# Slots of a hand-staged pipeline: 46 entries of the table AT are set to other numbers

## The reference

```
x = x + attn(norm(x))      # softmax((x*w_lhs)(x*w_rhs)^T) x, per sequence
x = x + ffn(norm(x))       # operands rounded to fp8 e4m3, 256x256 product in fp32, bf16 bias
x = x + mamba(norm(x))     # own layer norm; xz = xn W_in^T; conv over 4 taps; u = silu(xc)
                           # B, C = u W_x^T (16 each); delta = softplus(u W_dt^T)
                           # h_t = exp(delta A) h + delta u B ; y_t = sum_s h_t C ; 512 channels x 16 states
                           # out = (y + u D) silu(z) W_out^T
x = x + moe(norm(x))       # 8 experts, the top 2 by softmax; 352 hidden; one shared expert of 704
```

## Time and profile before

| | |
|---|---|
| median of three runs | 3336.52 us |
| profiled execution | 3335.78 us |
| its span, first to last instruction | 3334.1 us |
| first scan starts, last scan ends | 150.3 and 2665.2 us |
| turn 0 / turns 1 to 13 / turn 14 / turn 15 | 145.1 / 158.9 to 161.5 / 152.9 / 133.0 us |
| from the last scan to the end (experts) | 668.9 us |
| mean granted TensorE clock | 0.93 |

### The profile page before, as it was taken

One profiled execution on the slowest core, in us unless ns is written; L12 is line 12 of the kernel. 1 busy time (PEld: TensorE's weight loads), 2 busy tenths in 40 slices (PEclk: granted clock), 3 DMA queues, 4 the chain that ended last, 5 costly groups with the idle time before them and its releaser, 6 DMA issues. The chain is left out here.

```text
span 3334.1 us, 46771 instructions
## 1 busy us (share of the span) xinstructions
PE 2825.2 (85%) x12696; PEld 1879.2 (56%) x12697; DVE 2553.8 (77%) x4108; ACT 2075.7 (62%) x3786; POOL 2588.7 (78%) x2474
## 2 busy tenths in 40 slices
PE   4686979797979797888888888889787779999998
PEld 2444555555555555555565556555545447777776
DVE  3498999999999999999999898989898842222222
ACT  3577677776767676776767676777665414444443
...
GB/s 76 23 33 32 36 45 36 43 41 39 41 40 39 39 44 37 45 36 50 28 51 30 51 31 48 33 47 36 38 37 96 90 51 60 63 62 62 63 63 51
DMA packets 113899, 155.39 MB, mean 47 GB/s; under 512 B 15472, under 2 KB 73264, under 8 KB 113712
## 3 DMA queue, kind: packets, MB, share of 16 engines
...
## 5 line engine op out<-in xcount | busy, mean ns | idle before, releaser
L872 POOL TENSOR_TENSOR dbu<-du,bbc 128x512 f32<-128x512 f32 x1024 | 1292.4, 1280 | 58.5 <-DVE h L1440 51.2
L1440 DVE TENSOR_TENSOR_SCAN h<-bank,dbu 128x512 f32<-128x512 f32 x1024 | 1224.4, 1211 | 103.9 <-POOL dbu L872 52.1
L1082 ACT ACTIVATE bank<-region,amat 128x512 f32<-128x512 f32 x1024 | 697.2, 690 | 302.4 <-DVE h L1440 295.3
L665 PE MATMUL bank<-ident,h 128*128 128x128 f32 x4096 | 633.3, 292 | 225.5 <-DVE acc L1430 198.1
L665 PEld LDWEIGHTS bank<-ident,h 128*128 128x128 f32 x4096 | 507.6, 150 | 511.5 <-DVE acc L1430 204.4
L858 POOL TENSOR_TENSOR acc<-acc,hTc 128x512 f32<-128x512 f32 x480 | 609.3, 1270 | 98.9 <-ACT hTc L1066 97.9
L1607 POOL DMA_INDIRECT out<-ye,ids x136 | 213.6, 1570 | 348.3 <-DMA out<-ye,ids 313.2
L1066 ACT ACTIVATE hTc<-bank,cT 128x512 f32<-128x512 f32 x480 | 327.4, 682 | 240.6 <-PE bank L665 236.3
L1430 DVE SCALAR_TENSOR_TENSOR acc<-bank,cT,acc 128x512 f32<-128x512 f32 x544 | 395.8, 730 | 47.6 <-PE bank L665 45.3
L619 PE MATMUL bank<-x4T,w_su 128*128 128x512 f32 (+1 forms) x768 | 391.2, 613 | 10.7 <-DVE score L1305 10.7
L1643 DVE SCALAR_TENSOR_TENSOR gg<-gt,bank 128x352 f32<-128x352 f32 x136 | 71.0, 522 | 382.9 <-ACT gt L1577 382.9
...
## 6 DMA issues: line engine op xcount, KB each, us to landing
bbc<-b_scratch SPq DMA_DIRECT2D x256, 256.0 KB, 3.1
xe<-slots_in SPq DMA_DIRECT2D x136, 129.0 KB
...
out<-ye,ids POOLq DMA_INDIRECT x136
...
slots_in<-x,pos POOLq DMA_INDIRECT x128, 2.6
```

Source lines behind the costliest of these rows:

```text
L665: last = tr(scan[f"hT{s}.{t}"][:, m * P:(m + 1) * P], h[:, s % 2, m, t * P:(t + 1) * P], ident[:, :])
L872: g.tensor_tensor(dbu[:, n % 4, :], du[:, m, :], bbc[:, (b * NS + s) % NROW, :], ALU.mult).then_inc(S("dbu_ready"), 1)
L1082: f(db(n)[:, :], delta[:, 1 - par, m, :], ACT.Exp, scale=amat[:, m, s:s + 1]).then_inc(S("da_ready"), 1)
L1440: v.tensor_tensor_scan(h[:, s % 2, m, :], db(n)[:, :], dbu[:, n % 4, :], 0.0, ALU.mult, ALU.add)\
```

## The change

46 entries of AT get other values, most by one or two slots. Two lines of the table:

```diff
-            yT=(0, 0, 1, 2), y=(0, 0, 1, 1), uD=(2, 3, 3, 3), acc0=(1, 2, 2, 2), out=(4, 6), x3=(6, 9), stats5=12, rstd5=11, x4=13,
+            yT=(0, 0, 1, 2), y=(0, 0, 1, 1), uD=(2, 3, 3, 3), acc0=(1, 2, 2, 2), out=(4, 6), x3=(7, 10), stats5=12, rstd5=11, x4=14,
...
-            delta=(55, 56, 57, 60), stats1=4, rstd1=1, xn=8, xT=(9, 11), xl=(11, 12), scores=(15, 19, 21, 26), maxs=(18, 21, 24, 29),
+            delta=(54, 55, 56, 56), stats1=4, rstd1=4, xn=8, xT=(9, 11), xl=(11, 12), scores=(15, 19, 21, 26), maxs=(18, 21, 25, 29),
```

More of the change, by code:

```diff
@@ L306, in layers @@
         AT = dict(
-            yT=(0, 0, 1, 2), y=(0, 0, 1, 1), uD=(2, 3, 3, 3), acc0=(1, 2, 2, 2), out=(4, 6), x3=(6, 9), stats5=12, rstd5=11, x4=13,
-            x4T_pe=(14, 17), x4T=(14, 17), logit=18, lg=20, lexp=19, score=21, route=27, count=39, place=40,
-            ranks=(40, 43, 44, 45, 48, 49, 50, 52), g_pe=(20, 26, 30, 40, 47, 53), g=(22, 27, 32, 41, 49, 54),
-            gate=(24, 29, 34, 43, 51, 56), u_pe=(23, 25, 34, 42, 47, 54), up=(25, 29, 36, 45, 54, 56), d_pe=(51, 56), fin=(57, 62),
@@ L311, in layers @@
-            stats3=2, rstd3=1, res=2, r4=4, r4T_pe=5, r4T=1, in_x=(8, 10, 14, 17), tap=(11, 12, 17, 19), conv=(13, 15, 19, 21),
-            tanh=(13, 15, 21, 21), u=(16, 18, 23, 24), base=11, xBC_pe=24, bs=25, cT_pe=28, cT=32, in_z=(31, 37, 43, 51),
-            z=(33, 39, 46, 53), zs=(38, 42, 48, 55), dt_pe=(26, 33, 40, 49), raw=(30, 37, 44, 52), sp_exp=(32, 43, 49, 55), sp_ln=50,
-            delta=(55, 56, 57, 60), stats1=4, rstd1=1, xn=8, xT=(9, 11), xl=(11, 12), scores=(15, 19, 21, 26), maxs=(18, 21, 24, 29),
@@ L315, in layers @@
-            probs=(18, 21, 24, 29), probT_pe=(29, 35, 36, 38), probT=(31, 36, 38, 39), av=(41, 45), x1=(48, 52), stats2=52, rstd2=51,
-            xb=54, q=46, q_dve=56, qT_pe=57, qT=62, ffn_pe=(61, 63), ffn=(61, 63), x2=64, store=0, tags=(39, 53), q_round=55, q_nan=55,
-            q_fin=57)
+            yT=(0, 0, 1, 2), y=(0, 0, 1, 1), uD=(2, 3, 3, 3), acc0=(1, 2, 2, 2), out=(4, 6), x3=(7, 10), stats5=12, rstd5=11, x4=14,
+            x4T_pe=(14, 16), x4T=(14, 16), logit=17, lg=20, lexp=20, score=21, route=26, count=39, place=40,
@@ new lines, in layers @@
+            ranks=(42, 45, 45, 47, 50, 51, 52, 54), g_pe=(20, 26, 30, 40, 44, 50), g=(22, 27, 32, 41, 46, 51),
+            gate=(24, 29, 34, 43, 48, 53), u_pe=(23, 25, 33, 42, 44, 54), up=(25, 29, 36, 45, 51, 56), d_pe=(51, 56), fin=(58, 63),
+            stats3=2, rstd3=1, res=3, r4=4, r4T_pe=5, r4T=3, in_x=(8, 10, 15, 17), tap=(11, 12, 17, 19), conv=(13, 15, 19, 21),
+            tanh=(13, 15, 20, 21), u=(16, 17, 23, 24), base=12, xBC_pe=24, bs=25, cT_pe=29, cT=31, in_z=(31, 38, 45, 51),
+            z=(33, 40, 48, 53), zs=(38, 43, 50, 55), dt_pe=(26, 34, 40, 49), raw=(30, 38, 44, 52), sp_exp=(32, 44, 49, 55), sp_ln=51,
@@ L319, in layers @@
+            delta=(54, 55, 56, 56), stats1=4, rstd1=4, xn=8, xT=(9, 11), xl=(11, 12), scores=(15, 19, 21, 26), maxs=(18, 21, 25, 29),
+            probs=(18, 21, 24, 29), probT_pe=(30, 33, 34, 36), probT=(32, 34, 36, 37), av=(40, 47), x1=(46, 52), stats2=48, rstd2=51,
+            xb=54, q=50, q_dve=57, qT_pe=56, qT=62, ffn_pe=(63, 63), ffn=(63, 64), x2=64, store=0, tags=(40, 54), q_round=54, q_nan=56,
+            q_fin=58)
         END = 1000
```

## The result

The changed kernel takes 3368.32 us, the median of five runs (3366.18 to 3371.45), against 3336.83 us for five runs of the kernel before beside it: a ratio of 1.0095, 95% interval 1.0084 to 1.0107. It is slower by 31 us. The forecast was 3356, slower by 20, with a range of 3318 to 3378. The profiled execution took 3364.8 us, with a span of 3362.8.

The account below looks back on a forecast made before the run. Bound by a ring of stretches held by different engines, VectorE and GpSimd nearly equally busy. 13 turns by 1.4 us is 18, plus 1 each for turns 0 and 14: 3336 + 20 = 3356 us, range 3318 to 3378.

Parts of the forecast that it names:

- the rivals: Whole kernel: faster, 3311 to 3321 us, chance 0.28; no change, 3336, 0.15; slower by more, 3380, 0.14.
- 1. rstd1, 0: Head of the turn: scan 5 can start 1.79 us earlier, scan 6 cannot because ScalarE's chain holds it; gain 0.
- The rival "faster": Head of the turn: the removed wait counts in full, 1.79 us a turn, 3311 us (3321 with half the losses); chance 0.28.
- 2. x3, +0.6 a turn: Head: L1284 leaves the wait before scan 6 for VectorE's gapless stretch behind it, about 0.6 us a turn.
- 3. probT, base, in_x, tanh, x4 and the score: Units 33 to 35: L922 goes behind exp 33, freeing scan 33's small wait; scan 35 comes when it came, 0.
- 4. av0 and the bank, +1.0 a turn: Units 40 to 44: another TensorE step and a bank wait delay the transposes and GpSimd's add, 1.0 us on the path.
- 5. Dispatch and q, 0: Dispatch DMAs move later within GpSimd's gapless stretch; the later q chain removes VectorE's small wait for L927; both 0.
- 6. delta, +1.26 at dbu 60 to 63: End of the turn: the fourth L813 goes from behind dbu 63 to before dbu 60, making dbu 60 to 63 1.26 later.
- 7. ffn, -1.5: Tail: two transpose groups go ahead of L504, so the last 16 can begin after scan 63; some 1.5 us won.
- 6 and 7 nearly cancel: End of the turn: 1.26 us lost to the late L813, some 1.5 won in the tail.
- the signs that it named: Middle turn: scan 5 1.8 us earlier, scan 6 unmoved, waiting 2.9; dbu waits at scans 60, 61, 63; turns 161.7 us.
- The paragraph on a memory port: GpSimd product L866 beside VectorE's L1227: one more collision could cost 0.8 us a turn, 10 in all; only in the range.

Follow-up runs that it names:

- both rstd1 runs: Kernel before with only rstd1 moved from slot 1 to 4: 3337.72 us; changed kernel with rstd1 back at slot 1: 3368.49 us.
- the middle block: Kernel before with only the changed slots of probT, av, x1, gates and up products, z, dt, q, ranks and tags: 3380.28 us, ratio 1.012.
- the fillers: Eight 128x512 matmuls on constants in TensorE's idle stretch behind unit 12: on the changed kernel 3364.93 us, on the kernel before 3342.82 us.
- the single parts: Kernel before with one group of new slots each: rstd1 3337.72, x3 3352.38, ffn 3336.31, delta 3366.48, x4 with logit and in_x 3361.78, middle 3380.28 us.
- The run that should have filled it: Kernel before with delta's new slots plus two 128x384 matmuls on constants behind the transposes of r4: 3389.21 us, ratio 1.0154.

## Why the prediction was right

The direction, the places and most sizes held; the sum was 11 us short. At 3368.3 the time lies inside the wide range of 3318 to 3378, which was opened for the rivals, and 1 us above the forecast's own, 3345 to 3367. By its steps:

1. rstd1, 0: right. Scan 5 came 1.94 us earlier, scan 6 where it was, and both rstd1 runs are flat. The rival "faster" rested on this wait counting in full.
2. x3, +0.6 a turn: right in the whole change, +0.58 at scan 7. Alone it cost 1.3 a turn in its trace; its four turns of neither low stretch take 161.0 in the mean, 0.7 more than before, but they reach from 159.7 to 162.2.
3. probT, base, in_x, tanh, x4 and the score: the probT wait at unit 33 did vanish and scan 35 kept its distance. But the edits of x4 and in_x in this group, costed at 0, and of logit, which it doesn't name, put the second half of the first score behind four transposes and an input product. The prediction said, under its part 2, that L1176 moves "within stretches where VectorE has no idle or waits for others anyway". That sentence is the step that failed. It looked at VectorE's row and not at TensorE's, and not at its clock: the score's slack was less than what a longer low stretch takes. It cost 0.93 a turn, 12 us in all, as much as the gap between forecast and result. That the errors of steps 4 and 7 (-0.38 and +0.39 a turn) cancel is luck.
4. av0 and the bank, +1.0 a turn: in VectorE's row right, scan 51 is 1.03 later than scan 35 was; in GpSimd's, where I put it on the path, only 0.62 (2.13 of dbu 51 less the 1.51 of scan 35). GpSimd had swallowed some of the earlier delay, as its wait shows, 0.78 us where I expected 1.6.
5. Dispatch and q, 0: nothing measured speaks against it; it wasn't tried alone, only in the middle block.
6. delta, +1.26 at dbu 60 to 63: the shift of dbu 61 to 63 is 1.23, as forecast. dbu 60 is passed by two L813 and comes 2.46 later, which the prediction missed and which costs nothing seen: scan 60 waits for TensorE's transposes. Without delta the kernel is only 0.58 a turn faster, but between turns with the low clock in the same places it is 1.2, as forecast.
7. ffn, -1.5: L504 left the tail, the wait of turn 5 fell from 1.81 to 0.81, and the turn got 1.11 back in the mean from scan 63 to the next scan 0. Mis-sized by 0.4, because turn 5 was no pattern here: the 1.81 was read in a tail at 1.2 GHz. Before, six turns like it had a tail of 11.75 us, and the five with a tail at 2.4 GHz had 10.0 and the wait of 0.81 already. In the changed kernel the clock is low for at most 1.2 of the first 5 us of the tail, and in the pair of delta and ffn, where it is low for longer, the tail takes 10.0 all the same. So the new order takes away what the low clock cost, and wins 0 to 0.4 us in a tail at 2.4 GHz. That 6 and 7 nearly cancel was tested by the pair: 0.4 us a turn net.

Summed: 0.58 + 0.93 + 0.62 + 1.23 + 0.12 - 1.11 = 2.37 us a turn, the 0.12 being scan 63 against its dbu. The forecast had 0.6 + 0 + 1.0 + 1.26 + 0 - 1.5 = 1.4. Most of the signs that it named were there: scan 5 early and scan 6 in place, a wait of 3.50 us for ScalarE (2.9 forecast), a wait for dbu at scan 61 (in nine turns), a tail wait under 1.81. Scan 60 waits for TensorE instead (0.17 us in nine turns, 1.6 in the four with a low stretch at 145 us), scan 63 doesn't wait, and GpSimd's add waits 0.78 us and not 1.6. Turns were 162.6 rather than 161.7.

The paragraph on a memory port has no experiment, but the traces bound it. One L866 of each turn is long: 2.25 us in eight turns and 1.71 in five before, 2.25 in all thirteen after. That is 2.7 us in all and not 10, and the steps add up without it.

That TensorE's clock decides what an order costs, I did not consider at all, though the mean of 0.94 stood in the earlier trace rows. The Trainium skill (TensorE: Matmul & The Clock Gate, "Part 1: The HAM clock gate") says that the chip halves TensorE's clock when it has not been busy; the windows above and the fillers agree.

Open: why the early low stretch comes in some turns of the single parts and in none of the whole change or of delta with ffn. The traces show that it starts just behind an idle stretch of TensorE, 1.97 us in the turn shown; turn 6 of the same run has one of 1.49 us at the same place and before one of 1.50, and no low stretch behind it. The run that should have filled it filled another place.
